# Attention scatter of every second tile: four float32r matmuls and four transposes in place of sixteen float32 passes, gathers issued in pairs

## What is computed

```
Xv   = h @ W_val.T                      # values, per batch and node
attn = softmax over the edges of one source node (per batch, head)
Vt   = Xv[:, dst]                       # gather: a value row for each edge
Y    = segment_sum(attn[..., None] * Vt, src)   # scatter: sum the edges of each node
x    = x + Y @ W_out.T                  # project
```

## Time and profile before

| | before |
|---|---|
| time, median of 3 runs | 1282.31 us (1281.72 to 1283.64) |
| the profiled execution's own time | 1282.6 us |
| its span | 1280.9 us |
| mean granted PE clock | 0.993 |
| PE busy | 1223.2 us (95%) |
| DVE busy | 1013.9 us (79%) |
| ACT busy | 870.9 us (68%) |
| POOL busy | 333.9 us (26%) |

### The profile page before, as it was taken

How to read it: one execution, slowest core, us unless ns; L and a number is a source line. 1 busy time by engine, 2 the same in 40 slices (tenths; PEclk the granted TensorE clock), 3 DMA queues, 4 the chain that set the end, 5 groups by cost and what they waited for, 6 DMA issues and landing times.

```text
span 1280.9 us, 22499 instructions
## 1 busy us (share of the span) xinstructions
PE 1223.2 (95%) x7286; PEld 1017.2 (79%) x7286; DVE 1013.9 (79%) x2032; ACT 870.9 (68%) x1657; POOL 333.9 (26%) x738
## 2 busy tenths in 40 slices
PE   4888999999899998899999999999999899999998
PEld 4888996663398887689778887888898777778998
DVE  4786868987768885988788878887886699988664
ACT  4564768868668886877687768777776577773332
POOL 4775761000067440000000000000000466653331
PEclk9998999999999999999999999999999999999999
DMA  8000000000031110000000000000200300001212
GB/s 307 1 1 2 2 1 1 0 1 0 19 122 66 66 58 1 1 1 2 1 1 1 1 1 1 1 1 27 105 2 1 132 1 1 2 1 41 75 67 83
DMA packets 14635, 38.22 MB, mean 30 GB/s; under 512 B 1872, under 2 KB 3920, under 8 KB 13392
## 3 DMA queue, kind: packets, MB, share of 16 engines
q1 hardware_dynamic: 13152, 36.31, 7.3%
q10 hardware_dynamic: 1392, 0.74, 0.2%
HBM read 20.27 MB, written 16.78 MB: 29 GB/s over the span
## 4 chain that ended last, share of the span: by engine, by line
PE 52%; DVE 5%; ACT 2%; issue 1%; POOL 1%; POOLq 0%; DVEq 0%; ACTq 0%
PE bank L1091 7%; PE bank L1092 7%; PE bank L1093 7%; PE bank L1563 4%; PE bank L1106 4%; PE bank L1357 4%; PE bank L1102 4%; PE bank L1103 4%; PE bank L1345 4%; PE bank L1553 2%; PE bank L1571 2%; ACT gates L1121 1%; PE bank L1329 1%; PE bank L1247 1%; DVE Y L1176 1%
## 5 line engine op out<-in xcount | busy, mean ns | idle before, releaser
L1121 ACT ACTIVATE gates<-bank,lstm_bias 128x512 f32<-128x512 f32 (+1 forms) x504 | 301.6, 636 | 102.1 <-PE bank L1106 89.2
L161 ACT ACTIVATE l_h<-X,nmr,rstd 128x128 f32<-128x128 f32 (+1 forms) x512 | 209.9, 483 | 38.6 <-POOLq L155 25.9
L1091 PE MATMUL bank<-lstm_node_hi,Wih_hi 128*128 128x512 f32 (+1 forms) x408 | 149.4, 366 | 0.0
L1092 PE MATMUL bank<-lstm_node_hi,Wih_lo 128*128 128x512 f32 (+1 forms) x408 | 148.9, 365 | 0.0
L1093 PE MATMUL bank<-lstm_node_lo,Wih_hi 128*128 128x512 f32 (+1 forms) x408 | 148.9, 365 | 0.0
L130 POOL TENSOR_TENSOR l2r_sum<-l2r_st 128x8 f32<-128x8 f32 x16 | 4.2, 263 | 529.1 <-DVE l2r_st L111 529.1
L1102 PE MATMUL bank<-lstm_hid_hi,Whh_hi 128*128 128x512 f32 (+1 forms) x288 | 104.5, 363 | 4.0 <-DVE lstm_hid_hi L1181 3.8
L1106 PE MATMUL bank<-lstm_hid_lo,Whh_hi 128*128 128x512 f32 (+1 forms) x288 | 106.9, 371 | 0.0
L1103 PE MATMUL bank<-lstm_hid_hi,Whh_lo 128*128 128x512 f32 (+1 forms) x288 | 103.2, 358 | 0.0
L1126 ACT ACTIVATE gates<-lstm_cell 128x512 f32<-128x512 f32 (+1 forms) x144 | 83.7, 581 | 20.8 <-DVE lstm_cell L1168 20.5
L1093 PEld LDWEIGHTS bank<-lstm_node_lo,Wih_hi 128*128 128x128 f32 x408 | 77.1, 189 | 11.6
(11 more groups left out here) (248 smaller groups left out, 3275.4 us busy)
## 6 DMA issues: line engine op xcount, KB each, us to landing
x_spill<-X SPq DMA_DIRECT2D x32, 256.0 KB, 2.0
X<-x_spill SPq DMA_DIRECT2D x2, 4096.0 KB, 12.6
out<-X SPq DMA_DIRECT2D x32, 256.0 KB, 2.0
X<-in_x SPq DMA_DIRECT2D x7, 1024.0 KB, 16.1
X<-in_x SPq DMA_DIRECT2D x2, 512.0 KB, 7.2
w_raw<-in_WihT SPq DMA_DIRECT2D x1, 1024.0 KB, 6.1
w_raw<-in_WhhT SPq DMA_DIRECT2D x1, 1024.0 KB, 8.3
W<-in_L_W ACTq DMA_DIRECT2D x1, 192.0 KB, 3.0
```

Source lines behind the costliest of these rows:

```text
L161: last = act.activation(h[:, j, :], k.X[:, bass.ds(b0, TB), :][:, j, :], ACT.Relu, bias=k.nmr[:, bass.ds(b0, TB)][:, j:j + 1], scale=k.rst ...
L1091: pe.matmul(out, hi, x_high, start=True, stop=False)
L1092: pe.matmul(out, lo, x_high, start=False, stop=False)
L1121: act.activation(gate_of(it, g), k.bank[4 * s + g][:, 0:it.N], ACT.Tanh if g == GATE_G else ACT.Sigmoid, bias=k.lstm_bias[:, it.p - 1, g:g ...
```

## The change

Even tiles keep their path. For an odd tile t:

- `weighted_high` (ACT, two instructions) copies `Vw` to float32r `Wh`, and `weighted_low` (POOL, two instructions) writes `Wl = Vw - Wh`. Each chunk has its own semaphore count.
- `scatter_split` (PE) is 4 float32r matmuls of 512 columns with `S1` as the stationary operand and `Wh`, `Wl` as the moving ones. Its output is nodes by features.
- `untransposed` (ACT) copies that from PSUM to `Ys`; `turn_over` (PE) turns it over with 4 transposes into the same bank; `transposed` (ACT, the old copy to `YT`) follows.

PE's list for a pair of steps (t even) becomes `scatter(t)`, `project(t-1)`, `gather(t+2)`, `gather(t+3)`, softmax parts, `scatter_split(t+1)`, `project(t)`, `turn_over(t+1)`, softmax parts. ACT's becomes the copy of t-1, `weighted_high(t+1)`, the copy of t, `high(t+4)`, `high(t+5)`, exponential, `untransposed(t+1)`. DVE does the add of a tile ahead of the two `weighted`. POOL does `weighted_low(t+1)`, `low(t+4)`, `low(t+5)`.

```
+    def scatter_split(self, pe, t):
+        EC = self.k.E // P
+        for c in range(EC):
+            pe.wait_ge(self.wlo_done, t // 2 * EC + c + 1)
+            if c == 0:
+                self.wait(pe, self.YT_done, t, 2)
+            for part in (self.Wh, self.Wl):
+                last = pe.matmul(self.psY[1][:, :], self.e.S1[:, c, :], part[:, c, :, :],
+                                 start=c == 0 and part is self.Wh, stop=c == EC - 1 and part is self.Wl)
+        last.then_inc(self.Y_done, 1)
+
+    def turn_over(self, pe, t):
+        pe.wait_ge(self.Ys_done, t // 2 + 1)
+        for j in range(TB):
+            last = pe.transpose(self.psY[1][:, j * P:(j + 1) * P], self.Ys[:, j, :], self.k.ident[:, :])
+        last.then_inc(self.Yp_done, 1)
...
+    def weighted_high(self, act, t):
+        self.wait(act, self.Vw_done, t)
+        if t > 1:
+            act.wait_ge(self.Y_done, t // 2)
+        for c in range(self.k.E // P):
+            act.activation(self.Wh[:, c, :, :], self.Vw[t % self.W][:, c, :, :], ACT.Copy).then_inc(self.whi_done, 1)
+
+    def weighted_low(self, pool, t):
+        EC = self.k.E // P
+        for c in range(EC):
+            pool.wait_ge(self.whi_done, t // 2 * EC + c + 1)
+            pool.tensor_tensor(out=self.Wl[:, c, :, :], in0=self.Vw[t % self.W][:, c, :, :], in1=self.Wh[:, c, :, :],
+                               op=ALU.subtract).then_inc(self.wlo_done, 1)
+
+    def untransposed(self, act, t):
+        act.wait_ge(self.Y_done, t // 2 + 1)
+        act.activation(self.Ys[:, :, :], as_tile(self.psY[1]), ACT.Copy).then_inc(self.Ys_done, 1)
...
     def on_tensor(self, pe):
         for t in self.steps:
+            even = t % 2 == 0
             if there(t):
-                self.scatter(pe, t)
-            if there(t + 2) and t + 2 > 1:
-                self.gather(pe, t + 2)
+                (self.scatter if even else self.scatter_split)(pe, t)
+            if there(t - 1):
+                self.project(pe, t - 1)
+            if even:
+                for ahead in (t + 2, t + 3):
+                    if there(ahead) and ahead > 1:
+                        self.gather(pe, ahead)
+            if there(t) and not even:
+                self.turn_over(pe, t)
...
-            if there(t - 1):
-                self.project(pe, t - 1)
...
     def on_scalar(self, act):
         for t in self.steps:
-            if there(t + 3) and t + 3 > 1:
-                self.high(act, t + 3)
-            if there(t):
-                self.wait(act, self.Yp_done, t)
-                self.wait(act, self.O_done, t, 2)
-                act.activation(self.YT[t % 2][:, :, :], as_tile(self.psY[t % 2]), ACT.Copy).then_inc(self.YT_done, 1)
+            if t % 2 == 0:
+                if there(t - 1):
+                    self.transposed(act, t - 1)
+                if there(t + 1):
+                    self.weighted_high(act, t + 1)
+                if there(t):
+                    self.transposed(act, t)
+                for ahead in (t + 4, t + 5):
+                    if there(ahead):
+                        self.high(act, ahead)
+            elif there(t):
+                self.untransposed(act, t)
             if due(t, 6):
                 sm.exponential(act, due(t, 6))
...
     def on_pool(self, pool):
-        for t in range(2, self.tiles):
-            self.low(pool, t)
+        for t in range(-2, self.tiles, 2):
+            if self.there(t + 1):
+                self.weighted_low(pool, t + 1)
+            for ahead in (t + 4, t + 5):
+                if self.there(ahead):
+                    self.low(pool, ahead)
...
     def on_vector(self, dve):
         for t in self.steps:
-            if there(t + 2) and t + 2 > 1:
-                self.weighted(dve, t + 2)
             if there(t - 1):
                 self.wait(dve, self.O_done, t - 1)
                 xt = X[:, (t - 1) * TB:t * TB, :]
                 dve.tensor_tensor(xt, as_tile(self.psO), xt, ALU.add).then_inc(self.added, 1)
+            if t % 2 == 0:
+                for ahead in (t + 2, t + 3):
+                    if there(ahead) and ahead > 1:
+                        self.weighted(dve, ahead)
```

More of the change, by code:

```diff
@@ L1015, in stage_lstm_to_attend @@
     sc = Scores(k, ctx, HT, e, k.nc.sbuf_base - 8 * 4 * TW, w_at)
-    at = Attend(k, e, sc, out, gates_at, w_at + 7 * 4 * TW, gates_at + 4 * 4 * TW)
+    at = Attend(k, e, sc, out, gates_at, w_at + 7 * 4 * TW, gates_at + 4 * 4 * TW, gates_at + 8 * 4 * TW)
     groups = k.B // GROUP
@@ L1513, with __init__ @@
     W = 3
-    def __init__(self, k, e, sc, out, v_at, w_at, sm_at):
+    def __init__(self, k, e, sc, out, v_at, w_at, sm_at, split_at):
         self.k, self.e, self.out, self.attn, self.Xv = k, e, out, sc.scores, sc.Xv
@@ L1522, in __init__ @@
         self.YT = each(2, lambda s: at(f"at_yT{s}", [P, TB, P], w_at + (self.W * EC + s) * tile))
+        self.Wh, self.Wl = (at(f"at_w_{n}", [P, EC, TB, P], split_at + m * EC * tile, F32R) for m, n in enumerate(("hi", "lo")))
+        self.Ys = at("at_ys", [P, TB, P], split_at + 2 * EC * tile)
+        self.whi_done, self.wlo_done, self.Y_done, self.Ys_done = (k.sem(f"at_{n}") for n in ("whi", "wlo", "Y", "Ys"))
         self.vhi_done, self.vlo_done, self.V_done, self.Vw_done, self.Yp_done, self.YT_done, self.O_done, self.added, self.stored = (
@@ L1582, in low, with transposed @@
                            op=ALU.subtract).then_inc(self.vlo_done, 1)
+    def weighted_high(self, act, t):
[13 more added lines that the diff above has]
+        act.activation(self.Ys[:, :, :], as_tile(self.psY[1]), ACT.Copy).then_inc(self.Ys_done, 1)
+    def transposed(self, act, t):
+        self.wait(act, self.Yp_done, t)
+        self.wait(act, self.O_done, t, 2)
+        act.activation(self.YT[t % 2][:, :, :], as_tile(self.psY[t % 2]), ACT.Copy).then_inc(self.YT_done, 1)
     def weighted(self, dve, t):
```

## The result

The changed kernel takes 1277.12 us (median of 6, 1276.73 to 1279.15) against 1282.18 us for the kernel before in the same session: 5.1 us less, ratio 0.9959 with a 95% interval of 0.9949 to 0.9970. The forecast was 1278.0 us, within 1276.3 to 1281.6. Run again beside the experiments, the same kernel gave ratios of 0.9966 and 0.9967, so 4.2 to 5.3 us is what the executions support.

The account below looks back on a forecast made before the run. PE's own work was taken as the bound. Fifteen odd tiles gave -6.3 us; start +0.3, lateness +0.5, exponential +0.4, last split +0.95, end -0.18: together -4.3 from 1282.31, so 1278.0 us, range 1276.3 to 1281.6.

Parts of the forecast that it names:

- PE's work: In each odd tile, 16 records (1.79 us) give way to 4 float32r matmuls and 4 transposes (1.37): 0.42 us less.
- The rival of faster streaming: 12 float32r matmuls in a row on PE cost 0.215 us each, saving another 3.1 us: 1274.9 us; chance 0.03.
- The pairing priced at nothing: Grouping the gathers on PE neither costs nor saves time, since type changes showed no extra cost in the chain.
- The hand-laid pair: Timeline of all engines over one pair of tiles: 6.81 us, with POOL, ACT and DVE fitting and PE the bound.
- POOL's slack: In a pair, POOL's weighted_low chunks are ready 1.9 and 1.1 us before scatter_split on PE wants them.
- POOL becomes the bound: Rival: POOL's subtractions slow to 2.05 us each, PE loses 0.46 us per pair, giving 1284.9 us; chance 0.06.
- turn_over's lateness: PE's transposes wait for the copy Ys, weights 0.06 us late: 0.03 us for each of 15 tiles, 0.5 us in all.
- the exponential: In three pairs ACT's exponential, after high(t+5), pushes the copy Ys by another 0.13 us: 0.4 us in all.
- The cold restart: Rival: turn_over restarts PE cold each time, 15 x 0.3 = 4.5 us in place of 0.5: 1282.0 us; chance 0.15.
- The start: weighted(3) ahead of add_linear on DVE delays turn_in, so scatter(2) starts 0.3 us later, eating tile 1's gain.
- The end: Last pair: 0.95 us lost waiting for POOL's chunk 1 at scatter_split(31), 0.18 gained before project(31).
- ACT's order 0.3 us later: Rival: high(t+5) ends 0.3 us later per pair, delaying Ys and turn_over equally; gain gone, 1282.3 us; chance 0.05.

Follow-up runs that it names:

- the run with pairs alone: The changed kernel's new order of work with every tile scattered in the old way, against the kernel before: 1283.58 us, ratio 1.0004.
- the uncovered run: The changed kernel with turn_over(t) right behind scatter_split(t), ahead of project(t-1), so nothing covers the copy Ys: 1290.57 us, ratio 1.0059 to the kernel before.

## Why the prediction was right, by its own steps

**PE's work.** 0.42 us less for an odd tile was the forecast, 5.67/14 = 0.405 the measure. The split scatter came at 0.93 to 0.94 as priced; four transposes at 0.45 to 0.46, not 0.44. `S1` as the stationary operand costs what the gather's did, and the long float32r runs are no faster: the 8 matmuls of two gathers take 1.87, 0.234 each. The rival of faster streaming is out. The Trainium skill, "TensorE: Matmul & The Clock Gate", section "Back-to-back issue gap", has 216 ns as the gap of an isolated matmul of 512 columns, and 131 ns for a sustained stream; the trace agrees with neither for float32r, at 234 ns. The pairing priced at nothing is shown by the run with pairs alone.

**The hand-laid pair.** It held: PE's pair is 6.83 for 6.81, and POOL's first subtraction begins 1.2 us into the last pair, 1.3 in the layout. POOL's slack, 1.1 in the layout, measured 1.07 by loading POOL. The rival "POOL becomes the bound" was a real one: one more subtraction, or the order with single gathers, is enough to lose the whole gain.

**turn_over's lateness** (+0.5) and **the exponential** (+0.4) were the mis-sized terms. Both measured nothing. A weight load 0.04 us ahead of its matmul is in time; I had wanted 0.11 because unbroken streams of float32 records show that lead, and a lead that a queue happens to have isn't one that it needs. The exponential overlaps the end of the copy before it on ACT, and `at_ys` starts 0.20 us after project in those pairs as in the others. The cold restart, my second case with 0.15, was therefore wrong by kind: a restart costs 0.2 us where PE has really waited (the uncovered run), and at the transposes it never did.

**The start**: +0.3 forecast, +0.30 measured, with turn_in held by `add_linear` as said.

**The end**: -0.42 + 0.03 + 0.95 - 0.18 = +0.38 forecast, +0.34 measured.

The sum was -4.3, the stage gave -5.03; the difference is the 0.9 of the two terms above less 0.2 in the transposes (14 tiles at 0.405 in place of 0.42). No large errors cancelled each other in it. That the median fell by 5.1 in one session and by 4.4 to 4.8 in others is the measurement's own width. One rival's sum was rounded: with ACT's order 0.3 us later in each pair it is -4.3 + 4.5 = +0.2, so 1282.5 and not 1282.3.

**What I missed** is who pays at the shared port. I had asked whether DVE slows POOL, and had POOL's subtractions staying at 1.27; it is mostly POOL that holds up DVE's instructions with two operands in SBUF. The Trainium skill, "SBUF — State Buffer", section "Who interferes with whom", says that DVE and GpSimd share a pair of ports as an exclusive lock, that a DVE instruction with two SBUF inputs contends with a GpSimd one that reads SBUF, and that the order of issue decides who blocks. The trace agrees, but for its first overlap. POOL's two subtractions of the timeline above, seen one at a time, are

```profile
1195.86 1.32 POOL L1618 TENSOR_TENSOR at_w_lo<-at_w,at_w_hi 128x512 fp32r<-128x512 f32 x1 [1.61 <-ACT at_w_hi L1612]
...
1197.14 1.68 POOL L1618 TENSOR_TENSOR at_w_lo<-at_w,at_w_hi 128x512 fp32r<-128x512 f32 x1
```

The scan that began at 1196.14, inside the first, ended at 1197.72, 0.89 later than it would alone and 0.54 behind that subtraction's end. The second subtraction began inside this scan and took 0.4 longer than usual, and DVE's subtraction, begun inside it at 1197.76, ended 0.27 behind its end. Only POOL's first one, begun 0.25 before the end of a scan, lost no more than 0.05. DVE's multiplications and adds, with one operand in PSUM, keep their times: medians of 680 and 691 ns, 683 and 682 in the kernel before. That POOL's subtractions are the cause is shown by the runs that take them away (pairs alone, low halves on DVE), where the scans are back at 0.69; that it is the port is the page's account, which no run here separates from another coupling of the two engines.

## What to carry to other kernels

Where one engine is full, price an edit by that engine's records alone, then lay the others out by hand for one period and ask for each handover how much slack is left; the split paid only because the gathers in pairs gave POOL 1 us of it. When a wait is taken out at a start or an end, look at what the freed engine now runs into: here the microsecond gained was lost again at once through three DVE instructions that ran beside POOL's. When a profiled stretch comes out longer than the waits in it, read the granted clock there before looking for more waits: in the two runs with more work on POOL 1.6 and 1.5 us were the clock. Elementwise work of two SBUF operands is best kept from running on DVE and POOL at the same time; moving it from POOL to DVE, which had room, gave 0.75 us directly and made another 1.0 us reachable.

## What the runs showed of the hardware that I had not expected

- A DVE instruction with two SBUF operands (scan, subtract) beside a POOL subtraction took 1.58 for 0.69 us and 1.33 for 0.42; POOL's pair of subtractions 2.96 for 2.50.
- A weight load that starts 0.04 us before its matmul does not delay it; in unbroken float32 streams it starts 0.11 before.
- Behind PE's waits for POOL the granted clock was about 0.5 for 3 to 3.5 us in two places, and there 8 float32 records took 1.71 us in place of 0.89.
- POOL takes 1.25 us for a 128x512 float32 subtraction, from start to start, whether it writes the values' or the weighted halves.
